# Fetching x into SBUF by 32 row gathers from Pool in place of eight transfers from ACT's queue

## The reference

```
x = x + tanh(g_xattn[0]) * L0_xattn(layernorm(x), ctx)      # 16 heads, keys and values from ctx
x = x + tanh(g_ffn[0])   * L0_ffn(layernorm(x))             # 16 experts, top 4, and a shared one
x = x + tanh(g_xattn[1]) * L1_xattn(layernorm(x), ctx)      # causal over [ctx, x]
x = x + tanh(g_ffn[1])   * L1_ffn(layernorm(x))             # layer norm, ternary weights
```

## Time and profile before

| | us |
|---|---|
| time, median of 2 runs | 1782.1 |
| lowest and highest | 1780.25, 1783.94 |
| the profiled execution, first to last instruction (its span) | 1779.8 |
| first block in it, up to the first instruction of the second | 26.98 |

### The profile page before, as it was taken

How to read it: one execution, slowest core, us unless ns; L and a number is a source line. 1 busy time by engine, 2 the same in 40 slices (tenths; PEclk the granted TensorE clock), 3 DMA queues, 4 the chain that set the end, 5 groups by cost and what they waited for, 6 DMA issues and landing times. The chain is left out here.

```text
span 1779.8 us, 33359 instructions
## 1 busy us (share of the span) xinstructions
PE 1522.2 (86%) x9714; PEld 821.0 (46%) x9824; DVE 1312.2 (74%) x2968; ACT 651.2 (37%) x937; POOL 361.5 (20%) x372
## 2 busy tenths in 40 slices
PE   4799946999999999999968838989989899998776
PEld 2455523555555555555534413433434344343455
DVE  5999855877778777877678737877878778885375
ACT  0455521111111111111123423655656556656540
POOL 3433332211112121111014541111111111111110
PEclk7999967999999999999989956999999999999998
DMA  5011000000000000000006793344533445330002
GB/s 178 19 36 35 18 1 1 0 0 0 0 0 0 0 0 0 0 0 1 0 30 199 224 181 51 52 67 58 80 52 51 67 60 79 51 52 1 1 0 94
DMA packets 63206, 77.32 MB, mean 43 GB/s; under 512 B 6626, under 2 KB 42210, under 8 KB 63138
## 3 DMA queue, kind: packets, MB, share of 16 engines
q1 hardware_dynamic: 57938, 72.00, 20.9%
q10 hardware_dynamic: 5200, 4.33, 0.8%
HBM read 49.31 MB, written 26.61 MB: 43 GB/s over the span
## 5 line engine op out<-in xcount | busy, mean ns | idle before, releaser
L1451 DVE TENSOR_REDUCE small<-ps 128x1 f32<-128x352 f32 (+8 forms) x816 | 420.9, 568 | 115.8 <-PE ps L1511 111.2
L1433 ACT ACTIVATE region<-ps 128x1024 f32<-128x1024 f32 (+5 forms) x384 | 322.8, 880 | 240.3 <-PE ps L1543 239.8
L953 PE MATMUL ps<-region 128*128 (+1 forms) x1632 | 378.3, 382 | 8.1 <-issue 7.6
L1511 PE MATMUL ps<-region 96*128 96x128 bf16 (+8 forms) x1280 | 250.5, 288 | 37.5 <-DMA region<-v_parts 30.4
L785 ACT ACTIVATE region<-ps 128x512 f32<-128x512 f32 x136 | 81.2, 597 | 446.4 <-PE ps L957 284.5
L953 PEld LDWEIGHTS ps<-region 128*128 (+1 forms) x1632 | 158.9, 98 | 178.3 <-issue 15.8
L967 PE MATMUL ps<-region 128*128 (+1 forms) x1632 | 201.7, 273 | 21.1 <-DVE region L893 18.1
L1543 PE MATMUL ps<-region 99*128 99x512 bf16 (+5 forms) x896 | 203.0, 324 | 16.4 <-issue 14.5
L1558 PE MATMUL ps<-region 128*32 128x512 f32 (+5 forms) x1792 | 188.3, 491 | 18.1 <-POOL region L1402 12.1
L1511 PEld LDWEIGHTS ps<-region 96*128 96x128 bf16 x1280 | 102.5, 100 | 217.7 <-DVE small L1451 122.5
L1402 POOL TENSOR_SCALAR_AFFINE_SELECT region<-region 128x512 f32<-128x512 f32 (+2 forms) x160 | 87.1, 548 | 523.7 <-ACT region L1433 523.6
(11 more groups left out here) (198 smaller groups left out, 1700.1 us busy)
## 6 DMA issues: line engine op xcount, KB each, us to landing
region<-k_parts SPq DMA_DIRECT2D x96, 136.0 KB, 7.5
region<-q_parts SPq DMA_DIRECT2D x96, 128.0 KB, 6.8
v_parts<-region SPq DMA_DIRECT2D x16, 576.0 KB, 6.4
region<-v_parts SPq DMA_DIRECT2D x16, 576.0 KB, 11.2
k_parts<-region SPq DMA_DIRECT2D x24, 272.0 KB, 3.9
q_parts<-region SPq DMA_DIRECT2D x24, 256.0 KB, 3.5
x_sb<-in_x ACTq DMA_DIRECT2D x8, 512.0 KB, 9.4
region<-in_w13T SPq DMA_DIRECT2D x16, 256.0 KB, 3.0
```

What stands on the lines that cost most here:

```text
L953: ins = nc.tensor.matmul(o, w(wt, kh, half_), xt[:, kh, cols], start=n == 0, stop=n == 5)
L1433: nc.scalar.activation(dst, src, ACT.Exp, scale=SCALE).then_inc(s_exp, 1)
L1451: ins = nc.vector.tensor_reduce(nmp[:, qt, h0:h0 + nh, place], bank[:, 0:nh * nk].rearrange("p (h k) -> p h k", h=nh), AX.X, ALU.max)
L1511: ins = nc.tensor.matmul(bank[:, h * nk:(h + 1) * nk], qa[0:STACK, v, h0 + h, qt * P:(qt + 1) * P], ka[0:STACK, v, h0 + h, k0:k0 + nk], st ...
```

## The change

x is no longer loaded by ACT. Pool writes a list of token numbers with an iota, `token[p, t] = t*128 + p` (128 x 32, unsigned 32 bit), waits for it, and then issues 32 indirect DMAs, one a tile: number t reads column t of the list and fetches 128 rows of 1 KB, one into each partition of `x_sb[:, t, :]`. All of this stands ahead of Pool's memsets and selects in its queue. ACT waits for 32 x 16 instead of 8 x 16 on s_x at the end of the block.

```diff
+        token = view(small, "token", [P, NT], F32).bitcast(U32)
...
+            s_token = sem("token")
...
             @block.scalar
...
-                for c in range(2 * B):
-                    act.dma_start(x_sb[:, c * TC:(c + 1) * TC, :],
-                                  x[c * CH:(c + 1) * CH, :].rearrange("(t p) d -> p t d", p=P)).then_inc(s_x, 16)
                 act.wait_ge(s_gate, 5 * 16)
                 nc.scalar.activation(tg[:], tg[:], ACT.Tanh).then_inc(s_gate, 1)
-                act.wait_ge(s_x, 2 * B * 16)
+                act.wait_ge(s_x, NT * 16)

             @block.gpsimd
             def _(pool):
+                nc.gpsimd.iota(token[:], [[P, NT]], base=0, channel_multiplier=1).then_inc(s_token, 1)
+                pool.wait_ge(s_token, 1)
+                for t in range(NT):
+                    nc.gpsimd.indirect_dma_start(out=x_sb[:, t, :], out_offset=None, in_=x,
+                                                 in_offset=bass.IndirectOffsetOnAxis(ap=token[:, t:t + 1], axis=0)
+                                                 ).then_inc(s_x, 16)
                 nc.gpsimd.memset(ident[:], 0.0).then_inc(s_pself, 1)
```

## The result

| | us |
|---|---|
| time before, median of 2 runs | 1782.1 |
| time after, median of 2 runs (1817.99 to 1822.26) | 1820.1 |
| ratio, 95% interval | 1.0209 (1.0184 to 1.0234) |
| the profiled execution of after, its span | 1820.5 |
| first block in it, up to the first instruction of the second | 59.72 |

The change makes the kernel 38 us slower, 2.1%. A second comparison with more runs (6 of after, 17 of before, one chip) gives 1817.65 against 1782.73, ratio 1.0198 (1.0172 to 1.0223): 34.9 us, and an effect that sits right on the 2% line.

The account below looks back on a forecast made before the run. The first block's last engine was taken to bound the change: Pool's start, iota, code load, gathers, memsets and selects, then VectorE's tail and barrier, sum to 57.9 us against 26.98, +30.9, so 1813.0 us; range 1797 to 1842.

Parts of the forecast that it names:

- rival 1: First block, Pool's queue: one code load and gathers of 0.9 to 1.35 us, the forecast itself, 1813 us; chance 0.50.
- The first block sets it; Pool becomes last: First block: Pool's in-order queue, with gathers ahead of its selects, holds up VectorE and ends the block; +30.9 us.
- The start of the second block, 57.9: End of the first block: the summed terms put the second block's start at 57.9 us, against 26.98 before.
- The tanh, near 10.7: First block, ACT: with x's issues gone, table load and tanh follow the small load's landing and end at 10.7 us.
- The price of a gather: First block, Pool's queue: 1.2 us each, bounds 0.41 and 2.91, 38.4 us for all 32.
- The code load: First block, ahead of Pool's iota or behind its gathers: on the path, 9.0 us, between bounds 6 and 12.1.
- Rival 3: Pool's gathers: the list is read entry by entry, 2.91 us a gather, +85.6 us, 1867.7 us; chance 0.05.
- No second library: First block, Pool: gathers and selects share one code load; otherwise one more load and one back, 13 us.
- rival 4: First block, Pool: the gather's code is in another library than the selects, +43.9 us, 1826 us; chance 0.09.
- x's landing costs nothing: First block's end: the last gather has 9.0 us to land; if it took 9.4 it would cost 0.4 us.
- Later stages are only shifted: Behind the first block: x's layout is the same, so every later stage moves by the same amount, its length unchanged.
- rivals 2, 3 and 4: Pool's gathers: heavier, 1.35 to 2.1 us, chance 0.24; list read entry by entry, 0.05; code in another library, 0.09.

Follow-up runs that it names:

- experiment 2: The kernel before, x still by ACT, with 20 memsets of 128x2304 ahead of Pool's own in the first block and no gather: 1817.03 us, ratio 1.0204.
- Experiments 5 to 7: Kernel before, x by eight plain Pool transfers: 1784.4 us; changed kernel with 64 gathers of 64 rows: 1854.9 us; with 16 gathers of 2 KB rows: 1803.0 us.
- experiment 6: The changed kernel with the same rows fetched by 64 gathers of 64 rows: 1854.9 us.
- experiment 10: The kernel before with ACT's x transfers, SP's loads and ACT's small loads all waiting for Pool's last select: 1789.5 us.
- experiment 3: The changed kernel with iota and gathers moved behind Pool's memsets and selects: 1814.5 us, ratio 1.0181.
- experiment 8: The changed kernel with 16 gathers by Pool and the other half of x by four transfers from ACT's queue: 1793.0 us.
- experiment 5: The kernel before with x by eight plain 512 KB transfers from Pool's queue, ahead of its memsets, without a list: 1784.4 us (before 1784.6 beside it).

## Why the prediction was right, and where it was off

The mechanism, the direction and the range held: 1820.1 (1817.7 over more runs) lies in 1797 to 1842, and rival 1, one load and gathers of 0.9 to 1.35 us, is what happened. Point by point:

- *The first block sets it; Pool becomes last.* Right, shown by the 40.4 us hole of VectorE and by experiment 2.
- *The start of the second block, 57.9.* 59.72 measured. The terms: load 9.0, measured 8.4; gathers 38.4, measured 40.3 (32 x 1.254, the first two longer by 0.5 in all); iota and its wait 0.4, measured 0.6; the hops between Pool's memsets and selects and from Pool to VectorE (0.16 and 0.12) were not in the sum; memsets, selects, tail and barrier as in the sum.
- *The tanh, near 10.7.* It ended at 9.06. I put ACT's table load behind the landing of the small vector; it ran at 3.37, during the wait. In after this costs nothing, since VectorE waits for Pool.
- *The price of a gather.* 1.2 against 1.254 looks better than its reasoning was. I built it from a software operation of 1.01 us and a list read of 0.20. Experiments 5 to 7 show the make-up: 1.17 us fixed for an instruction and its gap where I had 1.01, and 0.08 for a list of 128 where I had 0.20, nothing for bytes. Two errors of opposite sign; the row of an unrelated operation hit the fixed part to 0.16 us by chance, and the bounds of 0.41 and 2.91 were all that the trace of before could give. Rival 3 (entry by entry) is refuted by experiment 6: 64 entries more cost 0.042 us. The Trainium skill's rule of about 102 cycles for each small read command (GPSIMD Engine Reference, Performance pitfalls for Q7 kernels) does not describe a gather's list, by the same number.
- *The code load.* Bounds 6 and 12.1 held. The cause that I suspected, x's traffic, is at most part of it: with x held back it was 10.4, and beside x's full traffic but without any issue of SP or ACT 7.1. The Trainium skill's 6 us for a first call (GPSIMD Engine Reference, Instruction dispatch) is near the 6.9 of experiment 10, where nothing ran beside it, and too low for every load that had issues beside it.
- *No second library.* Right: one MODIFY_POOL_CONFIG pair ahead of the first select (at 0.9 us, ahead of the iota), so rival 4 falls.
- *x's landing costs nothing.* Right in after, where the tail hid it; experiment 3, which takes the tail off, shows what stood behind it: 3.4 us, in about 1.5 of which x still moves.
- *Later stages are only shifted.* Right for the work. The total was 7.1 us over the forecast in the two runs, 4.7 in the six. 1.8 of it is the first block. The rest arises behind it and differs from execution to execution: +8.0 in one profile of the changed kernel, +4.5 in the next, -1.7 with the memsets of experiment 2, -1.9 in experiment 8. It goes with the clock: behind the first block TensorE was at half clock for 213.4 us in the kernel before and for 224.8, 221.2, 205.1 and 208.0 in these four. I had left +-3 us for the clock, in the first block's neighbourhood alone; the term that was too small is that one, since every stage has such stretches.
- *The chances.* Within 2% had 0.62, slower 0.37. The effect came out at 1.0209 and 1.0198, on the line. With a point forecast of 1.7%, the first block's own error of 1.8 us and a few us of clock decide which side it falls on; 0.62 to 0.37 was too sure. (The chances of rivals 2, 3 and 4 add up to 0.38, not 0.37.)

## What to carry to other kernels

Ask first in whose queue a new instruction stands and who waits behind it: 40 us of gathers and 42 us of memsets in the same place of Pool's queue cost this kernel the same, although Pool is busy only 22% of the time and the gathers use a third of the DMA engines. For instructions with a price of their own, count instructions: a gather by list costs about 1.25 us of Pool's queue whether it moves 64 or 128 rows, 1 or 2 KB each, so use full lists and long rows, and a plain transfer where the addresses are regular (0.79 us for 512 rows, from the same queue). And look at what the removed part was holding up: eight issues of x held ACT's queue for 11.9 us, and moving them to SP's idle queue is the one version here that gains clear of noise (0.2%). Plain transfers from Pool's queue freed ACT as early and gained nothing, because a 1 KB vector then landed late.

## What the runs showed of the hardware that I had not expected

- A gather's price does not depend on its rows: 0.907 us for 64, 0.949 for 128, 0.946 for 128 rows of 2 KB, each with 0.30 to the next.
- Pool's memsets hold up VectorE's casts far more than the L207 rows let me think, and gathers hardly do. The same eight casts took 1.70 us in the kernel before, 1.82 beside the first gathers of after, and 16.77 beside the memsets of experiment 2, while these took 2.02 to 2.04 us each, as one did elsewhere in the kernel before (2.02). The 16 writes of kbd took 4.75 us beside the iota and the first gathers of experiment 3 instead of 4.29. The row of experiment 2:

```profile
21.72 16.77 DVE L355 CAST maskb<-small 1x256 bf16<-1x256 f32 x8
```

- Pool's first select or iota needs a code load that shows as an idle stretch with "issue" alone. Memsets (experiment 2) and plain transfers (experiment 5) ran ahead of it without one. It took 6.7 to 7.1 us where SP and ACT issued nothing beside it (experiments 2, 5, 10) and 8.4 to 12.1 where they did.
